# GpSimd instead of ScalarE writes the normalised rows after attention

## The chip, the cores and the metric

The kernel is one program on one core of a Trainium2 chip. The metric is the device time of one execution in microseconds (us). A core has five engines that run their own instruction streams and meet at semaphores: TensorE (PE; PEld is its weight load), VectorE (DVE), ScalarE (ACT), GpSimd (POOL) and SyncE (SP), which here only issues DMAs.

## The reference, cut to what matters

Two blocks, each a cross attention and an expert layer, on x of 4 x 1024 rows of 256 and a context of 4 x 64 rows of 192:

```python
x = x + xattn0(_layernorm(x), ctx, mask, ...)      # 8 heads of 64
x = x + ffn0(_layernorm(x), Wr, W1, W2)            # top 1 of 8 experts, with a capacity
x = x + xattn1(_layernorm(x), ctx, ...)            # 16 heads of 64
x = x + ffn1(_layernorm(x), Wg, W11, W12, W2)      # top 2 of 8 experts, gated

def _layernorm(x, axis=-1, eps=1e-05):
    m = jnp.mean(x, axis=axis, keepdims=True)
    v = jnp.var(x, axis=axis, keepdims=True)
    return (x - m) / jnp.sqrt(v + eps)
```

The change concerns the second and the fourth `_layernorm`, those on the sum of x and attention's output. Their result is what the router reads and what is sent to the experts.

## The kernel before, in words

The 4096 rows are 32 tiles (NT) of 128 rows. `attention(p, layer, ...)` is called once for each layer. Each engine has a function in it that loops over the same counter t, from -8 to 36, and does in round t a different step for different tiles: a software pipeline whose order is written out by hand. In round t:

- PE (`tensor`) transposes the softmax of tile t (L691), the normalised input of tile t + 4 (L700) and the normalised result of tile t - 2 (L706), makes the scores of tile t + 3 (L719), the output of tile t (L739) and the router's logits of tile t - 2 (L745), and for every fourth tile counts ranks (L755 to L759).
- DVE (`vector`) adds the output to x for tile t - 1 (L1091), takes the row maxima of tile t + 2 (L1119) and the statistics of tile t - 1 and of tile t + 6 (L1123 to L1145), and runs small steps of routing between them.
- ACT (`scalar`) copies transposes out of PSUM (L773, L777, L780), takes the exponentials of tile t + 2 (L794, one instruction a head and a read of its sum), and last in the round, for tile t - 1, writes the normalised rows (L804): x times 1/std plus a bias.
- POOL (`gpsimd`) scales the softmax of tile t + 1 by the reciprocal of its sum (L832), in the second layer fetches the expert rows of tile t + 8 (L840), sends a finished tile to the experts' buffer by one indirect DMA in the first layer and two in the second (L816), and then makes var + eps (L852), its power of -1/2 (L854) and that bias, -mean/std (L857).

So in round t the rows of tile t - 1 go DVE, POOL, ACT, and are read by PE in round t + 1. In the first layer they go to `L_stage`, a ring of 12 tiles; in the second they overwrite x in place, once the store of x to the output (issued by SP, L635) has landed. The scatter of tile u is issued 10 rounds (second layer 9) after its round by `scattered_at`, tighter for the last tiles; from round NT - 3 on it stands behind the variance steps and not ahead of them. The experts' stage of the second layer starts inside the last rounds (`behind`), with the gate of `E_sg` on ACT.

Names in the rows: `L_prob` softmax, `L_mv` mean and variance, `L_rstd` 1/std, `L_nb` the bias, `L_got` fetched expert rows, `rows` the experts' buffer in memory, `L_rcp` reciprocal of the sums.

## Time and profile before

| | us |
|---|---|
| time, median of 3 runs (lowest to highest) | 1082.34 (1081.46 to 1084.64) |
| span of the profiled execution | 1076.3 |
| first attention, from its first scores to the last tile | about 40 to 200 |
| first experts | about 200 to 500 |
| second attention | about 500 to 740 |
| second experts | about 740 to 1076 |

The span runs from the first to the last instruction; the 6.0 us between it and the median are start and end of the execution, outside all instructions. No time of its own is given for the profiled execution, so its span plus these 6.0 us stands for it, which by this definition is the median. In the stretch 40 to 200 PE is busy 155.0 of 160.0 us, in 500 to 740 it is 235.3 of 240.0. In the second stretch ACT is busy 214.9 and POOL 171.6 us.

How to read it: a row of the timeline has the start, the duration, the engine, the line and the operands, and in brackets how long the engine stood idle before it and what ended that. Indirect DMAs count as busy for POOL, but the gaps between them are issue time, in which POOL does nothing else either.

### The profile page before, as it was taken

What the parts mean: (1) busy time and instruction counts of PE and PEld (TensorE: products, weight loads), DVE (VectorE), ACT (ScalarE), POOL (GpSimd) and SP (SyncE); (2) the same over time, 40 slices, a digit from 0 to 9 for tenths busy, and PEclk for the clock granted to TensorE, in tenths of its full rate; (3) what the DMA queues carried; (4) which work ended last, traced back from release to release, by engine and by line L of the source; (5) the groups of instructions that cost most, each with busy time, mean ns of one, the idle gap of its engine ahead of it and who ended that gap; (6) DMA issues with size and microseconds to landing.
All of it is one profiled execution on the core that took longest, in us unless ns stands there. A gap on an engine that the chain in (4) does not pass through costs nothing.

```text
span 1076.3 us, 24183 instructions
## 1 busy us (share of the span) xinstructions
PE 1022.2 (95%) x7550; PEld 945.6 (88%) x7550; DVE 715.1 (66%) x2216; ACT 660.2 (61%) x2446; POOL 514.3 (48%) x522
## 2 busy tenths in 40 slices
PE   6999999899999999988999999989999999999994
PEld 4688888699999999866999999889899999999994
DVE  6778886454554444475777777858967676677663
ACT  2788987454554444347999999886445454444441
POOL 1356776442223333324558888766634324333233
PEclk9999999799999999988999999999999999999997
DMA  9920000466667775500111222247898566875783
GB/s 313 345 92 21 31 26 31 152 244 224 218 234 244 244 263 186 173 20 16 36 40 65 79 74 70 91 138 248 238 307 233 129 193 164 291 210 116 215 259 34
DMA packets 95490, 169.71 MB, mean 158 GB/s; under 512 B 12322, under 2 KB 70308, under 8 KB 93860
## 3 DMA queue, kind: packets, MB, share of 16 engines
q1 hardware_dynamic: 79028, 142.33, 39.0%
q0 software_dynamic: 16368, 26.23, 11.2%
q8 instruction: 46, 0.75, 0.3%
q14 instruction: 48, 0.39, 0.1%
HBM read 150.67 MB, written 62.43 MB: 198 GB/s over the span
## 4 chain that ended last, share of the span: by engine, by line
PE 77%; DVE 8%; DMA 7%; ACT 3%; issue 3%; POOL 1%; SPq 0%; POOLq 0%; DVEq 0%; ACTq 0%
PE psum L1720 13%; PE psum L719 11%; PE psum L739 11%; PE psum L1302 10%; PE psum L1319 10%; PE psum L1774 5%; PE psum L691 3%; DMA out<-E_y,E_dest 3%; PE psum L392 2%; ACT L_prob L794 2%; DMA E_up_w<-up 2%; PE psum L745 2%; PE psum L355 1%; PE psum L706 1%; PE psum L1740 1%
## 5 line engine op out<-in xcount | busy, mean ns | idle before, releaser
L794 ACT ACTIVATE L_prob<-psum,L_neg_max 128x64 f32<-128x64 f32 x768 | 228.6, 361 | 4.7 <-DVE L_neg_max L1119 4.6
L794 ACT ACTIVATION_READ_ACCUMULATOR L_prob<-psum,L_neg_max 128x1 f32 x768 | 194.8, 256 | 0.0
L1720 PE MATMUL psum<-E_xT_hi,E_up_w 128*128 128x256 f32 x1024 | 187.7, 281 | 6.7 <-DMA E_up_w<-up 3.3
L2131 POOL DMA_INDIRECT out<-E_y,E_dest x64 | 104.9, 1639 | 166.0 <-DVE E_y L1989 69.0
L1720 PEld LDWEIGHTS psum<-E_xT_hi,E_up_w 128*128 128x128 f32 x1024 | 158.4, 188 | 9.2 <-issue 7.5
L1720 PE MATMUL psum<-E_xT_lo,E_up_w 128*128 128x256 f32 x512 | 142.7, 279 | 0.0
L1874 ACT ACTIVATE E_sg<-psum 128x256 f32<-128x256 f32 x128 | 48.5, 382 | 107.8 <-PE psum L1720 106.2
L832 POOL TENSOR_TENSOR L_prob<-L_prob,L_rcp 128x512 f32<-128x512 f32 (+1 forms) x64 | 94.3, 1474 | 42.2 <-DVE L_rcp L1083 40.8
L739 PE MATMUL psum<-L_n_hi,L_pT_hi 128*128 128x256 f32 x384 | 107.5, 280 | 3.4 <-DVE L_pT_lo L1126 3.4
L1360 ACT ACTIVATE E_h_hi<-psum 128x256 fp32r<-128x256 f32 (+1 forms) x128 | 55.6, 437 | 85.8 <-PE psum L1302 85.8
L739 PE MATMUL psum<-L_n_lo,L_pT_hi 128*128 128x256 f32 x384 | 106.6, 277 | 0.0
L739 PE MATMUL psum<-L_n_hi,L_pT_lo 128*128 128x256 f32 x384 | 106.5, 277 | 0.0
L1403 DVE SCALAR_TENSOR_TENSOR E_h_lo<-psum,E_h_hi 128x256 fp32r<-128x256 f32 (+1 forms) x128 | 62.6, 491 | 54.2 <-ACT E_h_hi L1360 53.6
L1720 PEld LDWEIGHTS psum<-E_xT_lo,E_up_w 128*128 128x128 f32 x512 | 96.1, 188 | 0.0
L1319 PE MATMUL psum<-E_w_hi,E_h_hi 128*128 128x256 f32 x320 | 90.0, 281 | 0.0
L1319 PE MATMUL psum<-E_w_lo,E_h_hi 128*128 128x256 f32 x320 | 89.4, 279 | 0.0
L1319 PE MATMUL psum<-E_w_hi,E_h_lo 128*128 128x256 f32 x320 | 89.4, 279 | 0.0
L719 PE MATMUL psum<-L_m_hi,L_xT_hi 128*128 128x512 f32 x192 | 82.9, 432 | 2.0 <-ACT L_prob L794 2.0
L1302 PE MATMUL psum<-E_xT_hi,E_w_hi 128*128 128x384 f32 (+1 forms) x256 | 78.8, 308 | 1.4 <-DVE E_xT_lo L1395 1.4
L1302 PE MATMUL psum<-E_xT_hi,E_w_lo 128*128 128x384 f32 (+1 forms) x256 | 78.8, 308 | 0.0
L1302 PE MATMUL psum<-E_xT_lo,E_w_hi 128*128 128x384 f32 (+1 forms) x256 | 78.7, 308 | 0.0
L1952 DVE TENSOR_TENSOR E_hf<-psum,E_sg 128x256 f32<-128x256 f32 x128 | 53.5, 420 | 37.9 <-ACT E_sg L1874 37.8
(278 smaller groups left out, 3120.8 us busy)
## 6 DMA issues: line engine op xcount, KB each, us to landing
E_up_w<-up SPq DMA_DIRECT2D x26, 2048.0 KB
E_w<-in_w SPq DMA_DIRECT2D x16, 1024.0 KB, 7.2
E_w<-in_w SPq DMA_DIRECT2D x29, 512.0 KB
E_half_up_w<-up SPq DMA_DIRECT2D x28, 512.0 KB, 6.1
E_xin<-rows SPq DMA_DIRECT2D x32, 260.0 KB, 3.4
E_raw<-in_w SPq DMA_DIRECT2D x16, 512.0 KB, 7.0
up<-E_raw_hi SPq DMA_DIRECT2D x16, 512.0 KB, 6.5
up<-E_raw_lo SPq DMA_DIRECT2D x16, 512.0 KB, 3.7
```

The source lines that it names most:

```text
L719: mm = e.matmul(bank, a[:, (t + 3) % 2, c, :], m[:, b, c, q * 512:(q + 1) * 512], start=(layer == 1 and c == 0 and j == 0), stop=(c == KC ...
L739: mm = e.matmul(o, a[:, r, :], m[:, b, r, :], start=(r == 0 and j == 0), stop=(r == PR - 1 and j == 2))
L794: last = e.activation(prob[q][:, h * KEYS:(h + 1) * KEYS], scores_ps(t)[:, h * KEYS:(h + 1) * KEYS], ACT.Exp, bias=nmx[:, q, h, :], accum_ ...
L832: e.tensor_tensor(pr, pr, rc[:, q, :, :].to_broadcast([P, H, KEYS]), ALU.mult).then_inc(s_p, 1)
L1302: mm = q.matmul(bank, a[par][:, c, m * P:(m + 1) * P], x[:, c, c0 * P:(c0 + cn) * P], start=(k == 0), stop=(k == 3 * KC - 1))
L1319: mm = q.matmul(bank, a[:, h, m, c * P:(c + 1) * P], w[par][:, m, :], start=(k == 0), stop=(k == 3 * FC - 1))
L1360: q.activation(h_hi[:, h, m, 0:cn * P], ps[:, UP_BANK + m % 4, 0:cn * P], ACT.Relu).then_inc(s_hhi, 1)
L1403: q.scalar_tensor_tensor(h_lo[:, h, m, 0:cn * P], ps[:, UP_BANK + m % 4, 0:cn * P], 0.0, h_hi[:, h, m, 0:cn * P].bitcast(F32), ALU.max, AL ...
L1720: mm = q.matmul(bank, up_w[wpar(i, par)][:, half, w, c, m * P:(m + 1) * P], x[:, c, :], start=(k == 0), stop=(k == 3 * KC - 1))
L1774: mm = q.matmul(ps[:, Y_BANK + c, 0:D], a[:, par, m, c * P:(c + 1) * P], w[:, b, m, :], start=(k == 0), stop=(k == 3 * FC - 1))
L1952: q.tensor_tensor(hf[:, m, :], ps[:, UP_BANK + m, T1:2 * T1], sg[:, m, :], ALU.mult).then_inc(s_hf, 1)
L2131: q.indirect_dma_start(p.out[:, :], bass.IndirectOffsetOnAxis(ap=dest[:, par, c, :], axis=0), y[:, par, c, :], None, compute_op=ALU.add).t ...
```

## The change

For each of the 64 tiles, POOL's third small instruction (the bias, 128x1) becomes the pass over the rows itself, 128x256: subtract the mean, multiply by 1/std. ACT's pass and the bias tile go. The waits for the place that is written (in the first layer the ring slot's scatter, in the second the store of x) move with the pass from ACT's queue to POOL's. PE gets one more wait, in the first layer's round NT - 2: the banks of the last scores are about to be reused there, and until now ACT's pass told that its exponentials had been taken.

```diff
@@ attention: tensor
+            if ahead and t == NT - 2:
+                need(e, s_exp, NT)
@@ attention: scalar
-            if ok(t - 1):
-                i = t % 4
-                need(e, s_nb2, t)
-                if layer == 0:
-                    need(e, s_scat[(t - 1) % RING], 16 * ((t - 1) // RING))
-                else:
-                    need(e, s_store[(t - 1) % 4], 16 * ((t - 1) // 4 + 1))
-                e.activation(rows2(t - 1), p.x[:, t - 1, 0:D], ACT.Identity, bias=nb2[:, i:i + 1],
-                             scale=rs[:, i, 0:1]).then_inc(s_xf, 1)
@@ attention: gpsimd
                 if ok(t - 1):
                     need(e, s_rs, nrs(t))
-                    e.tensor_scalar(nb2[:, i:i + 1], mv[:, i, 0, 0:1], -1.0, rs[:, i, 0:1],
-                                    ALU.mult, ALU.mult).then_inc(s_nb2, 1)
+                    if layer == 0:
+                        need(e, s_scat[(t - 1) % RING], 16 * ((t - 1) // RING))
+                    else:
+                        need(e, s_store[(t - 1) % 4], 16 * ((t - 1) // 4 + 1))
+                    e.tensor_scalar(rows2(t - 1), p.x[:, t - 1, 0:D], mv[:, i, 0, 0:1], rs[:, i, 0:1],
+                                    ALU.subtract, ALU.mult).then_inc(s_xf, 1)
```

POOL's queue in a middle round of the second attention, before (the number behind a buffer's name tells its copies apart; in brackets the semaphores waited for):

```order
L852 TENSOR_SCALAR L_var_eps<-L_mv 128x2 [waits mean_var1,mean_var2]
L854 TENSOR_TENSOR L_rstd<-L_var_eps,half 128x2 [waits var_eps]
L857 TENSOR_SCALAR L_nb_150<-L_mv,L_rstd 128x1 [waits rstd]
L832 TENSOR_TENSOR L_prob_138<-L_prob_138,L_rcp 128x1024 [waits reciprocal]
L840 DMA L_got<-rows,row 128x256 [waits combined]
L816 DMA rows<-x,L_row_167 35072x260 [waits xf,routing]
```

and in the same round now:

```order
L844 TENSOR_SCALAR L_var_eps<-L_mv 128x2 [waits mean_var1,mean_var2]
L846 TENSOR_TENSOR L_rstd<-L_var_eps,half 128x2 [waits var_eps]
L853 TENSOR_SCALAR x<-x,L_mv,L_rstd 128x256 [waits x_stored3,rstd]
L824 TENSOR_TENSOR L_prob_137<-L_prob_137,L_rcp 128x1024 [waits reciprocal]
L832 DMA L_got<-rows,row 128x256 [waits combined]
L808 DMA rows<-x,L_row_165 35072x260 [waits xf,routing]
```

One instruction has changed its size, from one column to 256, and waits for a store as well; the order is the same. A second scatter follows in both.

ACT's queue in the same stretch, before:

```order
L794 ACTIVATE L_prob_139,L_sum<-psum,L_neg_max 128x64 x15
L804 ACTIVATE x<-x,L_nb_150,L_rstd 128x256 [waits x_stored0,neg_mean2]
L773 ACTIVATE L_pT_hi<-psum 128x1024 [waits pT]
L777 ACTIVATE L_xT_hi<-psum 128x256 [waits xfT,xT]
L780 ACTIVATE L_xfT<-psum 128x256 [waits xfT]
```

and now:

```order
L795 ACTIVATE L_prob_138,L_sum<-psum,L_neg_max 128x64 x15
L774 ACTIVATE L_pT_hi<-psum 128x1024 [waits pT]
L778 ACTIVATE L_xT_hi<-psum 128x256 [waits xfT,xT]
L781 ACTIVATE L_xfT<-psum 128x256 [waits xfT]
```

The pass between the exponentials and the copy of the transposed softmax is gone, and with it ACT's only wait for POOL in a round. DVE's and SP's queues and the order of PE's are as they were.

## Rows read from the trace of the kernel before

**Rows 1.** The chain that ended last, second attention: start, us, what.

```profile
573.06 0.93 PE psum L691 x8
...
574.20 0.32 PE psum L706 x2
...
668.27 0.94 PE psum L691 x8
```

**Rows 2.** PE's waits ahead of L706, first attention: total us, times.

```profile
ACT L_stage L804: 2.6, 9
```

**Rows 3.** POOL's waits in the stretch 40 to 200: total us, times, longest.

```profile
POOL L_var_eps L852 <- DVE L_mv L1145: 33.7, 26, 2.4
```

**Rows 4.** POOL's timeline over a round of the second attention, and a later row.

```profile
572.00 0.22 POOL L852 TENSOR_SCALAR L_var_eps<-L_mv 128x2 f32<-128x2 f32 x1
572.30 0.72 POOL L854 TENSOR_TENSOR L_rstd<-L_var_eps,half 128x2 f32<-128x2 f32 x1
573.14 0.26 POOL L857 TENSOR_SCALAR L_nb<-L_mv,L_rstd 128x1 f32<-128x1 f32 x1
573.44 1.90 POOL L832 TENSOR_TENSOR L_prob<-L_prob,L_rcp 128x1024 f32<-128x1024 f32 x1
575.51 1.07 POOL L840 DMA_INDIRECT L_got<-rows,row  x1 [0.17 <-issue]
576.88 1.00 POOL L816 DMA_INDIRECT rows<-x,L_row  x1 [0.30 <-DVE L_r L879]
578.19 0.97 POOL L816 DMA_INDIRECT rows<-x,L_row  x1 [0.30 <-issue]
579.23 0.23 POOL L852 TENSOR_SCALAR L_var_eps<-L_mv 128x2 f32<-128x2 f32 x1
...
667.10 0.23 POOL L852 TENSOR_SCALAR L_var_eps<-L_mv 128x2 f32<-128x2 f32 x1
```

**Rows 5.** Groups by line, shapes apart: count | busy us, mean ns | idle before.

```profile
L832 POOL TENSOR_TENSOR L_prob<-L_prob,L_rcp 128x1024 f32<-128x1024 f32 x32 | 60.9, 1904 | 33.6 <-DVE L_rcp L1083 32.8
L1440 POOL TENSOR_TENSOR E_raw_lo<-E_raw,E_raw_hi 128x1024 fp32r<-128x1024 f32 x16 | 38.4, 2403 | 76.6 <-ACT E_raw_hi L1369 70.1 <-DMA up<-E_raw_lo 6.6
L832 POOL TENSOR_TENSOR L_prob<-L_prob,L_rcp 128x512 f32<-128x512 f32 x32 | 33.4, 1043 | 8.6 <-DVE L_rcp L1083 8.0
L857 POOL TENSOR_SCALAR L_nb<-L_mv,L_rstd 128x1 f32<-128x1 f32 x64 | 17.3, 270 | 7.1
L339 POOL MEMSET L_vd<- 128x4096 f32 x1 | 3.5, 3512 | 0.0
```

**Rows 6.** ACT's waits in the stretch 515 to 740: total us, times, longest.

```profile
ACT x L804 <- POOL L_nb L857: 11.5, 18, 4.1
ACT x L804 <- DMA out<-x: 1.2, 1, 1.2
```

**Rows 7.** The chain again, at 196 and at 699 us.

```profile
196.49 0.50 ACT L_stage L804
...
698.78 0.58 POOL L_rstd L854
...
699.77 0.61 ACT x L804
```

**Rows 8.** POOL's timeline at the first attention's last tile.

```profile
193.73 0.57 POOL L854 TENSOR_TENSOR L_rstd<-L_var_eps,half 128x1 f32<-128x1 f32 x1
```

**Rows 9.** PE's timeline at the same place and at 722 us.

```profile
197.12 0.66 PE L706 MATMUL psum<-ident,L_stage 128*128 128x128 f32 x2 [0.60 <-ACT L_stage L804]
...
722.26 0.41 PE L706 MATMUL psum<-ident,x 128*128 128x128 f32 x2 [0.37 <-ACT x L804]
```

**Rows 10.** DVE's timeline: one small step away from L832 and beside it.

```profile
635.58 0.19 DVE L880 TENSOR_TENSOR L_sh<-L_lg,L_r 128x32 f32<-128x32 f32 x1
...
724.48 1.64 DVE L880 TENSOR_TENSOR L_sh<-L_lg,L_r 128x32 f32<-128x32 f32 x1
```

**Rows 11.** Busy us of each engine in one stretch, granted clock, DMA share.

```profile
735.00:745.00 10.00, 10.00 (x96) 10.00 (x96) 7.23 (x22) 6.24 (x17) 5.25 (x7) 1.00 0.54 150
```

More of the change, by code:

```diff
@@ L510, in attention @@
     rs = small("rstd", [P, 4, 2])
-    nb2 = small("nb2", [P, 4])
     if layer == 1:
@@ L556, in attention @@
     s_bn1, s_ag1, s_bn2, s_ag2 = S("stats1"), S("mean_var1"), S("stats2"), S("mean_var2")
-    s_eps, s_rs, s_nb2 = S("var_eps"), S("rstd"), S("neg_mean2")
+    s_eps, s_rs = S("var_eps"), S("rstd")
     s_xn, s_xT, s_xThi, s_xTlo = S("xn"), S("xT"), S("xT_hi"), S("xT_lo")
@@ L1171, in attention @@
     st.EARLY_TABLE, st.PLAN_STEPS = EARLY_TABLE, PLAN_STEPS
-    st.done = {s: NT for s in (s_bn1, s_ag1, s_bn2, s_ag2, s_nb2, s_xn, s_xT, s_xThi, s_xTlo, s_sim, s_mx, s_exp, s_rcp, s_p,
+    st.done = {s: NT for s in (s_bn1, s_ag1, s_bn2, s_ag2, s_xn, s_xT, s_xThi, s_xTlo, s_sim, s_mx, s_exp, s_rcp, s_p,
                                s_pT, s_pThi, s_pTlo, s_out, s_res, s_xf, s_xfT, s_xfTc, s_lgp, s_lg)}
```

## The prediction

> **What bounds the kernel now.** I read first the chain of work that ended last, in order of time, over both attentions. In the second it is one PE group after another, round upon round: L691 starts at 573.06 and, 13 rounds later, at 668.27 [rows 1], so a round is 95.21 / 13 = 7.32 us, PE's own work with next to no wait in it. In the first attention it reads the same. Next I asked who PE waits for ahead of L706, the transposes of the rows in question: 2.6 us in 9 waits in the first attention [rows 2], and in the second at single places late in it. That is all PE loses to ACT's pass today, and so about all that a pass finished sooner can give back. ACT is off this path, and its 64 passes of 0.6 us are hidden.
>
> Then POOL, which takes the work. In the first attention it has room: it stood 33.7 us over 26 rounds, 1.3 us in each, waiting for DVE's statistics [rows 3]. In the second, in the rounds that hold a fetch and two scatters, it has none: from 572.00 to 579.23 each instruction follows the last with only issue gaps [rows 4], 7.23 us of work in a round of 7.32; from 572.00 to 667.10 are 13 rounds of 7.315. POOL is full there, 0.09 us a round below PE. This is where the change is decided.
>
> **The length of the new pass, X.** No row has a two-operation tensor_scalar of 256 columns on POOL. Its fixed part is in L857, the same instruction on one column: 0.27 us [rows 5]. For the columns there are three slopes. A memset runs 4096 columns in 3.51 us, 0.86 ns each, and nothing that reads and writes should be faster: 0.27 + 256 x 0.86 ns = 0.48 us at least. The two-input multiply L832 goes from 1.043 us at 512 columns to 1.904 at 1024, 1.68 ns a column: 0.69 us. The two-input subtract into fp32r takes 2.403 us for 1024 columns, 2.35 ns each: 0.87 us, the upper end. The pass has one input and plain fp32 output, so I stand near the low end, for the second operation a little above it: X = 0.55 us. The Trainium skill's page GPSIMD Engine Reference, section Engine selection, bears on this: two-input elementwise operations cost GpSimd about twice VectorE's time and one-input ones run roughly at line rate; its section on the performance per element gives 1.03 cycles at 1.2 GHz for bodies of at most two operations. By this X would be 0.49, and the sum below 0.9 us lower. The same page's section 7 speaks against the change: an fp32 dependent chain, as subtract then multiply is, would cost 4 cycles an element. That would be 0.85 us on top of the fixed part and X = 1.12; no row here shows such a slope, the steepest being 2.35 ns.
>
> **Removed on ACT:** 64 passes and their waits for POOL (in the second attention 11.5 us in 18 waits [rows 6]). They are beside PE's work: ACT's next step, L773, needs PE's L691, which ends after the exponentials anyway (L691 runs from 573.06 to 573.99 [rows 1]). Worth 0 in itself. What the passes delay is L706, next.
>
> **Rows sooner for PE.** Today, at 698.78, L_rstd takes 0.58, L_nb and the pass follow, and the rows are there at 700.38 [rows 7]: 1.02 us after L_rstd. In the change it is 0.11 (the gap from L854 to L857 at 573.02 to 573.14 [rows 4]) plus X, 0.66 us. So 0.36 us sooner wherever this chain is what PE waits for.
> - First attention: 8 waits of L706, 2.0 us together (2.6 [rows 2] less the 0.60 of the one at 197 [rows 9]), 0.25 each in the mean, so under the 0.36; all but part of the longest goes: -1.7.
> - The wait at 196: ACT does its pass at 196.49 [rows 7] only because it is behind other work; POOL's L_rstd ended at 194.30 [rows 8]. PE waits 0.60 there, and the whole chain to the last scatters and the experts' first rows hangs on it: -0.5, with a little left for what is late next, the rank counts.
> - Second attention: at 699.77 -0.35; at 722 ACT's pass stands behind its exponentials and PE waits 0.37 [rows 9], which goes whole: -0.37.
> Sum -2.9 us. POOL's own round in the first attention grows by X - 0.27 = 0.28, and the 1.3 us of idle time hide it.
>
> **POOL's full rounds.** Each grows by X - 0.265 from 7.23 to 7.515 us [rows 4], against PE's 7.30 without its few small waits. PE does not feel it at once. At 573 the rows would be ready at 573.02 + 0.11 + 0.55 = 573.68, and L706 wants them at 574.20 [rows 1] less 0.05 of signalling: 0.47 in hand. After that PE gets a new wait of 0.21 ahead of L706 in each round. There are 14 such rounds (9 to 23; from round 24 on there is no fetch, which takes 1.37 us out of POOL's round, and POOL idles again): 14 x 0.215 - 0.47 = +2.5 us. In general that is 14 (X - 0.335) - (1.02 - X). What is queued behind the longer pass is L832, whose result PE needs only a round later, with 5 us in hand (575.34 against 573.06 + 7.32), and the fetch and scatters, which nobody awaits in these rounds. PE's time lost here doesn't come back, as PE has no idle time to give.
>
> **The waits that move.** In the second attention the pass waits for the store of x. Only once did ACT wait for it, 1.2 us at the last tile [rows 6]; elsewhere the store has landed in time. POOL will wait that about 1 us instead, with the scatters of tiles 28 and 29 and then the first adds of experts' output behind it. Those adds wait for DVE's E_y anyway, which covers it: 0, or 1 us if that cover is gone. PE's new wait for s_exp is for exponentials finished a round before: 0.
>
> **A rule against it.** DVE's small L880 takes 0.19 us normally and 1.64 when it starts inside an L832 [rows 10]: two engines on SBUF can hold each other off. The Trainium skill's page SBUF — State Buffer, section Who interferes with whom, gives the reason: a DVE instruction with two SBUF inputs shares GpSimd's read port, and the second to issue blocks until the first finishes; the trace agrees. In the full rounds the pass and the shifted L832 (now ending about 0.7 us later) fall beside DVE steps that read PSUM or one SBUF operand, and the next with two SBUF inputs, L1134, comes just behind. DVE also waits for ACT's sums in each round, which absorbs a hit. I count 0, with up to +2 in the range.
>
> **Sum:** -2.9 + 2.5 = -0.4 us on 1076.3 + 6.0, which gives 1081.9; I say 1082.0.
>
> **The rivals.**
> - *GpSimd becomes the bound in earnest (slower).* The pass runs at the slope of L1440 [rows 5], X = 0.87. The full rounds give 14 x 0.535 - 0.15 = +7.3; of the gains only 1.7 stay (0.8 in the first attention, 0.5 at 196, 0.37 at 721). Sum +5.6: 1088. With X = 0.69 it is 4.6 - 2.7 = +1.9. It costs more than 3.2 us from X = about 0.76 on. For it: subtract-then-multiply may be two steps of a loop. Against: one input. Were every column to wait for both operations in turn, at a slope of 3.3 ns that no row here has, X would be 1.12 and the time 14 x 0.785 + 0.1 = 11.1 later less 1 or so of gains, 1092; I give that 0.03 of this rival's 0.25. (That is what the rule on dependent chains in the Trainium skill's page GPSIMD Engine Reference, section 7, would make of the pass.)
> - *ACT's freedom pays at the seam (faster).* Around 727 to 741 us ACT stands in front of its pass, up to 4.1 us for POOL and 1.2 for the store [rows 6], and the gates of the second experts, E_sg, queue behind it; right after them the chain goes through DVE. If DVE's work there starts 2.5 us sooner and X = 0.48 (-1.5), the time is 1078.3. For it: the waits are real. Against: PE is busy 10.00 of 10.00 us from 735 to 745 [rows 11], so its PSUM results, not ACT, time these steps.
> - *The full rounds don't bind and only gains stay:* if the issue gaps around the DMAs shrink as the pass grows, -2.9: 1079.4. Against: the 0.30 us gap is the same from row to row [rows 4].
>
> **How the numbers follow.** The forecast, X between 0.48 and 0.75, has 0.60: 1080.8 to 1085. GpSimd as the bound 0.25. The seam 0.09, gains alone 0.06. Within 0.3%, 3.2 us, about what a measurement of this kernel can tell from no change, lies the forecast; of the last case's 1079.4 nearly all is inside too, of the slower rival's a little. Faster 0.12, same 0.62, slower 0.26. The range of 8 in 10 is 1079.5 to 1088.0.
>
> **What would show it.** The new POOL pass at 0.5 to 0.6 us, 64 times. Rounds of the second attention from 573 to 668 of 7.5 us, with waits of PE ahead of L706 on POOL of about 0.2 us in each; POOL without idle time there. In the first attention no waits ahead of L706, and the first experts starting about 2 us sooner. ACT's idle time moved ahead of L773. Wrong would be: a pass above 0.75 us, full rounds that stay at 7.32, or a change of more than 1 us in the stretch after 745.

## The result, and the profile after

The changed kernel takes **1102.18 us** (median of 4 runs, 1098.03 to 1103.07), the kernel before, run beside it, 1083.49 us (4 runs, 1081.46 to 1088.41). The ratio is 1.0158, 95% interval 1.0126 to 1.0190: by the ratio 17 us slower, by the two medians 18.7. The prediction was 1082.0 with a range of 1079.5 to 1088.0, and "same" as the likeliest. It is wrong, in sign and in size.

The first thing to read is the new pass itself. The two groups of the changed kernel, shapes apart (count | busy us, mean ns | idle before), are:

```profile
L853 POOL TENSOR_SCALAR x<-x,L_mv,L_rstd 128x256 f32<-128x256 f32 x32 | 40.9, 1279 | 5.0 <-DMA out<-x 1.7
L853 POOL TENSOR_SCALAR L_stage<-x,L_mv,L_rstd 128x256 f32<-128x256 f32 x32 | 39.5, 1233 | 3.5
```

X is 1.23 us, not 0.55, and above the upper bound of 0.87 that the prediction took from the rows of before. Most of the loss follows from it. The full round of the second attention that answers to [rows 4] now reads on POOL (start us, us, instruction):

```profile
574.45 0.25 POOL L844 TENSOR_SCALAR L_var_eps<-L_mv 128x2 f32<-128x2 f32 x1
574.78 0.72 POOL L846 TENSOR_TENSOR L_rstd<-L_var_eps,half 128x2 f32<-128x2 f32 x1
575.62 1.23 POOL L853 TENSOR_SCALAR x<-x,L_mv,L_rstd 128x256 f32<-128x256 f32 x1
576.82 1.90 POOL L824 TENSOR_TENSOR L_prob<-L_prob,L_rcp 128x1024 f32<-128x1024 f32 x1
578.89 1.30 POOL L832 DMA_INDIRECT L_got<-rows,row  x1 [0.18 <-issue]
580.50 1.01 POOL L808 DMA_INDIRECT rows<-x,L_row  x1 [0.30 <-DVE x L878]
581.81 0.97 POOL L808 DMA_INDIRECT rows<-x,L_row  x1 [0.30 <-issue]
582.81 0.26 POOL L844 TENSOR_SCALAR L_var_eps<-L_mv 128x2 f32<-128x2 f32 x1
```

There is again no idle time but the issue gaps, and the round is 8.36 us here and 8.18 in the mean of the 14 such rounds, against 7.31 before. The chain, which went from one PE group to the next [rows 1], now goes through POOL (start us, us, what):

```profile
583.16 0.72 POOL L_rstd L846
583.99 1.24 POOL x L853
585.27 0.44 PE psum L705 x2
...
600.40 1.24 POOL x L853
601.68 0.44 PE psum L705 x2
...
616.69 1.24 POOL x L853
617.97 0.44 PE psum L705 x2
```

Two rounds lie between these PE groups: 585.27 to 601.68 to 617.97, 16.4 and 16.3 us. In between the chain runs over PE's scores and output, DVE's steps and POOL's two scatters. From 572 to 690 us PE's matmuls wait for POOL ahead of L705 14 times, 8.6 us together; before, the same stretch shows no wait of theirs. Over the whole kernel the idle time of PE and its weight load ahead of that line reads

```profile
POOL x L853: 25.5, 33
POOL L_stage L853: 7.7, 21
```

where before it was 2.6 us in 9 waits in the first attention [rows 2]. (Idle time of matmuls and of weight loads is added up here, so one gap can count twice.) Shares of the chain were PE 77%, DVE 8%, POOL 1% and are now:

```profile
PE 67%; DVE 13%; POOL 7%; issue 5%; DMA 4%; ACT 3%; POOLq 0%; DVEq 0%; SPq 0%; ACTq 0%
```

In the first attention POOL's wait for DVE's statistics was 33.7 us in 26 waits before [rows 3]; from 40 to 200 us it is now 15.3 us in 19 waits. Of the two rounds below the first has 0.40 us of it left, the second nothing:

```profile
122.92 0.23 POOL L844 TENSOR_SCALAR L_var_eps<-L_mv 128x2 f32<-128x2 f32 x1 [0.40 <-DVE L_mv L1141]
123.23 0.72 POOL L846 TENSOR_TENSOR L_rstd<-L_var_eps,half 128x2 f32<-128x2 f32 x1
124.06 1.23 POOL L853 TENSOR_SCALAR L_stage<-x,L_mv,L_rstd 128x256 f32<-128x256 f32 x1
125.27 1.03 POOL L824 TENSOR_TENSOR L_prob<-L_prob,L_rcp 128x512 f32<-128x512 f32 x1
126.48 1.10 POOL L808 DMA_INDIRECT rows<-L_stage,row  x1 [0.18 <-issue]
127.61 0.40 POOL L844 TENSOR_SCALAR L_var_eps<-L_mv 128x2 f32<-128x2 f32 x1
```

**Where the time went.** Four places of the timeline divide the span. "First experts" and "second experts" are the starts of the experts' first transposes of E_xin on PE; "24 rounds" runs from the first L_var_eps of two columns in the second attention to the last L_rstd of two columns, 24 rounds later; "experts' length" is from the first to the last start of the second experts' matmuls with E_up_w. All in us; a second trace of each of the two kernels (see the experiments) stands in the table too. A row is one execution, and that can lie 10 us from its kernel's median: the traced run of "one operation" took 1083.79 us, the fastest of five with a median of 1093.64.

| kernel | first experts | 24 rounds | second experts | experts' length | span |
|---|---|---|---|---|---|
| before | 214.0 | 176.5 | 715.1 | 334.8 | 1076.3 |
| before, second trace | 213.1 | 176.5 | 710.9 | 330.9 | 1068.5 |
| after | 218.5 | 188.3 | 729.8 | 339.6 | 1095.3 |
| after, second trace | 219.3 | 188.2 | 730.6 | 346.5 | 1104.9 |
| one operation | 214.1 | 184.5 | 719.4 | 337 | 1082.0 |
| constants | 217.4 | 186.4 | 730.4 | 344 | 1100.5 |
| two halves | 226.7 | 193.5 | 747.6 | 340 | 1113.5 |
| second attention only | 214.5 | 188.3 | 725.9 | 344 | 1096.2 |
| extra pass beside | 214.4 | 191.6 | 729.0 | 345 | 1100.7 |
| VectorE, both | 212.0 | 177.9 | 713.4 | 339.5 | 1082.8 |
| VectorE, first only | 214.9 | 176.4 | 715.3 | 344 | 1087.6 |
| first attention only | 219.1 | 176.8 | 720.6 | 336.0 | 1082.9 |
| softmax shared | 218.4 | 179.9 | 721.2 | 334.0 | 1081.3 |
| last seven tiles only | 213.7 | 176.5 | 711.9 | 332.9 | 1071.9 |

Of the 19.0 us between the first two spans, 4.5 come in the first attention, 11.8 in the 24 rounds, and 4.8 in the second experts' stretch; the rest of the kernel gives 2.1 back. The first two are sharp: the 24 rounds repeat within 0.1 us from trace to trace. The start of the first experts lies between 213.1 and 214.5 us in the five traces with the first attention of before, between 218.4 and 219.3 in the four with that of after. The experts' length is not sharp: it moves by 4 us between two traces of before and by 7 between two of after, and "VectorE, first only", whose second attention is that of before, has 344.

### The profile page after: what moved, and what is told of

It is laid out like the page before. It is cut to its first block, busy times and chain, and to the rows that moved or that the text cites. A ratio compares the mean times of both kernels' runs of the same rounds, so it can differ in the third digit from the quotient of the medians.

```text
span 1095.3 us, 24120 instructions
## 1 busy us (share of the span) xinstructions
PE 1024.7 (94%) x7550; PEld 942.4 (86%) x7550; DVE 722.8 (66%) x2216; ACT 627.3 (57%) x2382; POOL 579.4 (53%) x522
## 4 chain that ended last, share of the span: by engine, by line
PE 67%; DVE 13%; POOL 7%; issue 5%; DMA 4%; ACT 3%; POOLq 0%; DVEq 0%; SPq 0%; ACTq 0%
PE psum L1716 13%; PE psum L1298 10%; PE psum L1315 10%; PE psum L718 7%; PE psum L740 7%; PE psum L1770 6%; DMA out<-E_y,E_dest 3%; ACT L_prob L795 2%; PE psum L355 2%; DVE L_neg_max L1115 2%; POOL rows L808 2%; PE psum L392 2%; DVE L_pT_lo L1122 2%; POOL L_rstd L846 1%; PE psum L690 1%
## 5 line engine op out<-in xcount | busy, mean ns | idle before, releaser
L824 POOL TENSOR_TENSOR L_prob<-L_prob,L_rcp 128x512 f32<-128x512 f32 (+1 forms) x64 | 94.1, 1470 | 23.7 <-DVE L_rcp L1079 23.7
L774 ACT ACTIVATE L_pT_hi<-psum 128x512 fp32r<-128x512 f32 (+1 forms) x64 | 52.0, 813 | 75.5 <-PE psum L690 75.5
L1430 POOL TENSOR_TENSOR E_w_lo<-E_w,E_w_hi 128x2048 fp32r<-128x2048 f32 x8 | 38.9, 4865 | 76.7 <-ACT E_w_hi L1339 76.7
```

Source lines behind the costliest of these rows:

```text
L774: e.activation(flat(pT_hi[:, :, :]), pT_ps(), ACT.Copy).then_inc(s_pThi, 1)
L824: e.tensor_tensor(pr, pr, rc[:, q, :, :].to_broadcast([P, H, KEYS]), ALU.mult).then_inc(s_p, 1)
```

## The experiments

Two theories stood against each other at first. By **occupancy**, POOL has no room in its rounds, so any longer instruction there lengthens the round, whatever it computes. By **latency**, the rows themselves come later than by the bias on GpSimd and the pass on ScalarE, so PE's transposes wait for them, and other work on POOL doesn't matter. Beside them stood the question what makes the pass 1.23 us long, and whether VectorE could have done it.

**One operation.** The mean is not subtracted, so the rows are only scaled.

```diff
-e.tensor_scalar(rows2(t - 1), p.x[:, t - 1, 0:D], mv[:, i, 0, 0:1], rs[:, i, 0:1],
-                ALU.subtract, ALU.mult).then_inc(s_xf, 1)
+e.tensor_scalar(rows2(t - 1), p.x[:, t - 1, 0:D], rs[:, i, 0:1], None,
+                ALU.mult).then_inc(s_xf, 1)
```

> The pass on GpSimd with one operation in place of two: multiply by 1/std, the mean is not subtracted (left out of the computation; it is near 0). My theory T1: the pass took 1.23 us, not 0.55, because the two operations on an element are done one after the other on each column, 3.8 ns a column; with one of them it goes to about half of that, 0.27 + 256 x 1.9 ns = 0.75 us, and the time to within 3 us of before (1082 to 1088). Rival T2: the cost is that of a read and a write of fp32 with scalars from memory, whatever the operations; the pass stays at 1.2 us and the time at the changed kernel's 1098 to 1103.

Measured: 1093.64 us, ratio 1.0081 (1.0060 to 1.0102). The pass is

```profile
L853 POOL TENSOR_SCALAR x<-x,L_rstd 128x256 f32<-128x256 f32 x32 | 31.5, 985 | 4.3 <-DMA out<-x 1.1
L853 POOL TENSOR_SCALAR L_stage<-x,L_rstd 128x256 f32<-128x256 f32 x32 | 30.1, 941 | 3.3
```

0.29 us shorter in the first attention: so much is the second operation worth together with its per-partition operand, the mean. In the second attention it is 0.94 as well, except for one of 2.16 us at the end, which lifts the mean to 0.985. Neither theory of the expectation, 0.75 or 1.2 us, holds, and even one operation takes more than the prediction's upper bound for two. The time, some 9 us above before, is not within the 3 us that were expected. The first attention now loses nothing (first experts at 214.1), the 24 rounds lose 8.0 us. So the first attention does hide a pass of 0.94 us; it does not hide 1.23.

**Constants.** Two operations, with 0.0 and 1.0 in place of the mean and the reciprocal; the rows are not normalised.

```diff
-e.tensor_scalar(rows2(t - 1), p.x[:, t - 1, 0:D], mv[:, i, 0, 0:1], rs[:, i, 0:1],
+e.tensor_scalar(rows2(t - 1), p.x[:, t - 1, 0:D], 0.0, 1.0,
                 ALU.subtract, ALU.mult).then_inc(s_xf, 1)
```

> Both operations stay, but with the constants 0.0 and 1.0 in place of the per-row mean and 1/std (the rows are not normalised). T1 (the two operations one after the other): the pass stays near 1.2 us and the time near that of the changed kernel. T3: what is slow is taking two scalars per row from memory; then the pass falls to 0.5 to 0.7 us and the time to within 3 us of before.

Measured: 1099.35 us, ratio 1.0115 (1.0070 to 1.0160). The pass takes

```profile
L853 POOL TENSOR_SCALAR x<-x 128x256 f32<-128x256 f32 x32 | 35.6, 1112 | 4.3 <-DMA out<-x 1.5
L853 POOL TENSOR_SCALAR L_stage<-x 128x256 f32<-128x256 f32 x32 | 34.7, 1085 | 2.8
```

so the two per-partition operands are worth 0.15 us of the 1.23 (again without the last pass, 1.90 us here). With 0.07 for one operand the second operation alone is some 0.22 us, an estimate from these two kernels. T3, a fall to 0.5 to 0.7, is wrong. The rows, and so the routing, are others here and in "one operation"; what is compared are the pass and the rounds.

**Two halves.** The pass in two instructions of 128 columns.

```diff
-e.tensor_scalar(rows2(t - 1), p.x[:, t - 1, 0:D], mv[:, i, 0, 0:1], rs[:, i, 0:1],
-                ALU.subtract, ALU.mult).then_inc(s_xf, 1)
+for c in range(2):
+    h = slice(c * P, (c + 1) * P)
+    last = e.tensor_scalar(rows2(t - 1)[:, h], p.x[:, t - 1, h], mv[:, i, 0, 0:1], rs[:, i, 0:1],
+                           ALU.subtract, ALU.mult)
+last.then_inc(s_xf, 1)
```

> The pass in two instructions of 128 columns each, the same result. It gives slope and fixed part: if the fixed part is the 0.27 us of the one-column instruction and the slope 3.8 ns, each half takes 0.75 us and the pair 1.5. GpSimd's full rounds in the second attention then go from 8.17 to 8.4 or 8.5 us, and by 14 full rounds and some in the first attention the kernel is 5 to 8 us slower than the changed one (T1: GpSimd's occupancy is the bound). If instead the fixed part is large (0.7 us or more), each half takes nearly 1 us and the kernel is over 12 us slower. If GpSimd's occupancy is not the bound, the time stays.

Measured: 1115.95 us, ratio 1.0291 (1.0267 to 1.0314). Each half:

```profile
L855 POOL TENSOR_SCALAR x<-x,L_mv,L_rstd 128x128 f32<-128x128 f32 x64 | 52.7, 831 | 3.4 <-DMA out<-x 0.2
L855 POOL TENSOR_SCALAR L_stage<-x,L_mv,L_rstd 128x128 f32<-128x128 f32 x64 | 50.9, 803 | 3.3
```

From 128 to 256 columns the pass grows by (1233 - 803) / 128 = 3.36 ns a column, and 1.233 - 256 x 0.00336 = 0.37 us is fixed. (The one-column instruction took 0.27 [rows 5], so the line is not quite straight.) The full rounds are 8.51 us, the 24 rounds 5.2 us longer than in the changed kernel, the first experts start 8.2 us later. By the ratios that is some 14 us in all, where 5 to 8 were expected; what was left too small is the first attention. The prediction said of a slope of 3.3 ns that no row had it; the steepest there was 2.35 [rows 5]. The Trainium skill's page GPSIMD Engine Reference, section 7, gives 4 cycles an element to an fp32 dependent chain, which the prediction put at X = 1.12 with its own fixed part of 0.27; the trace agrees with the size of that slope. That such a chain is the cause is not shown: the pass with constants has the same two operations in turn, and with the same fixed part its 1.085 us give 2.8 ns a column, the single operation's 0.94 give 2.2 (estimates from these rows). The same page's section Engine selection, by which one-input operations run roughly at line rate, and its 1.03 cycles an element, from which the prediction worked out 0.49, do not agree: even with one operation the pass takes 0.94.

**Second attention only.** ScalarE and the bias are back in the first attention.

```diff
# ScalarE's pass
-if ok(t - 1):
+if ok(t - 1) and layer == 0:
# GpSimd
+if layer == 0:
     e.tensor_scalar(nb2[:, i:i + 1], mv[:, i, 0, 0:1], -1.0, rs[:, i, 0:1], ALU.mult, ALU.mult).then_inc(s_nb2, 1)
+else:
+    need(e, s_store[(t - 1) % 4], 16 * ((t - 1) // 4 + 1))
+    e.tensor_scalar(rows2(t - 1), p.x[:, t - 1, 0:D], mv[:, i, 0, 0:1], rs[:, i, 0:1], ALU.subtract, ALU.mult).then_inc(s_xf, 1)
```

> The change in the second attention alone; the first attention is as before. Of the 19 us, my reading of the two traces puts 4.5 in the first attention and the rest from 500 us on: then this kernel is 13 to 15 us slower than before, with the first experts' first transposes at 214 us as before. If the first attention's loss were larger than it looks because its delay is made good or doubled later, it would come out below 11 or above 18.

Measured: 1097.54 us, ratio 1.0098 (1.0071 to 1.0125). First experts at 214.5, as before; the 24 rounds 188.3, as in the changed kernel. The second attention has its loss without the first. By the ratio the time is 10.6 us above before (7.7 to 13.6), below the 13 to 15 that were expected, which the interval just reaches.

**Extra pass beside.** The kernel before, with its bias and ScalarE's pass, and on GpSimd, for 28 tiles of the second attention, one more pass of the new kind over a constant tile, which nobody waits for.

```diff
     e.tensor_scalar(nb2[:, i:i + 1], ...).then_inc(s_nb2, 1)
+    if layer == 1 and t < NT - 3:
+        e.tensor_scalar(scratch[:, :, :], p.ident[:, None, :].to_broadcast([P, 2, P]), mv[:, i, 0, 0:1], rs[:, i, 0:1],
+                        ALU.subtract, ALU.mult)
```

> The kernel before, with ScalarE's pass and GpSimd's small bias kept, and in the second attention (28 of its 32 tiles) one more GpSimd pass of the same form, 128x256 subtract and multiply, that reads a constant tile and writes scratch nobody reads. It stands behind the bias, so the rows for TensorE are not made later by it directly. T1 (GpSimd's occupancy is the bound in the full rounds): the pass takes 1.23 us, a full round 8.2 + 0.3 us (the bias stays in it), and the kernel is 11 to 15 us slower than before. T4 (what costs is the longer way from 1/std to the rows, 1.34 us in place of 1.02, round by round): under 3 us slower.

Measured: 1101.72 us, ratio 1.0162 (1.0102 to 1.0222). The extra pass, whose result goes nowhere, takes as long and lengthens the rounds to 8.42 us:

```profile
578.45 0.27 POOL L858 TENSOR_SCALAR L_nb<-L_mv,L_rstd 128x1 f32<-128x1 f32 x1
578.69 1.24 POOL L861 TENSOR_SCALAR L_scratch<-ident,L_mv,L_rstd 128x256 f32<-128x256 f32 x1
579.90 1.91 POOL L833 TENSOR_TENSOR L_prob<-L_prob,L_rcp 128x1024 f32<-128x1024 f32 x1
```

The 24 rounds take 191.6 us, 15.1 more than before, 3.3 more than in the changed kernel, which has no bias of 0.27 us in its 14 full rounds (3.8 us). This decides for occupancy and against latency in the second attention: the rows come from ScalarE as ever, and the loss is there. The time, 17.5 us above before by the ratio (11.0 to 24.0), is more than the 11 to 15 that were expected; in the trace the experts' length is 345 too, 10 above the first of before.

**VectorE, both attentions.** VectorE writes the rows right behind its own reciprocal; neither ScalarE's pass nor the bias is left.

```diff
# VectorE
     e.reciprocal(rc[:, q, :, :], sm[:, q, :, :]).then_inc(s_rcp, 1)
+if ok(t - 2):
+    u, i = t - 2, (t - 1) % 4
+    need(e, s_rs, nrs(t - 1))
+    ...
+    e.tensor_scalar(rows2(u), p.x[:, u, 0:D], mv[:, i, 0, 0:1], rs[:, i, 0:1], ALU.subtract, ALU.mult).then_inc(s_xf, 1)
# GpSimd and ScalarE
-e.tensor_scalar(nb2[:, i:i + 1], ...)
-e.activation(rows2(t - 1), ...)
```

> A version that might beat both: VectorE writes the rows, behind its reciprocal, one instruction of 128x256 like its L_xn (0.41 us), and neither ScalarE's pass nor GpSimd's bias is left. The way from 1/std to the rows is 0.1 + 0.41 us against 1.02 before, GpSimd's full round falls from 7.23 to 6.93 us, and VectorE's round grows by 0.33 us, of which it has 1 us and more idle. T1 and T4 both expect 1 to 4 us faster than before, by the small waits of TensorE ahead of its transposes. Rival T5: VectorE's later maxima and differences delay TensorE, or its serial stretch from 724 to 768 us grows by some passes: 1 to 5 us slower.

Measured: 1089.61 us (12 runs), ratio 1.0036 (1.0004 to 1.0069). The gain that was expected isn't there; the time is inside the range of rival T5. On VectorE the same pass takes a third of the time or less:

```profile
L1079 DVE TENSOR_SCALAR x<-x,L_mv,L_rstd 128x256 f32<-128x256 f32 x32 | 14.0, 438 | 0.9 <-POOL L_rstd L846 0.7 <-issue 0.2
L1079 DVE TENSOR_SCALAR L_stage<-x,L_mv,L_rstd 128x256 f32<-128x256 f32 x32 | 12.4, 387 | 0.0
```

One pass of 1.99 us lifts the first mean; the middle one is 0.33 us there and 0.38 into L_stage. The first experts start at 212.0, 2.0 us sooner; the 24 rounds take 177.9, 1.4 more than before. So VectorE could carry the work at a small cost, 0.4 to 7.5 us by the interval, and no gain showed. PE is busy 196.1 of the 200 us from 510 to 710, before 198.5. What makes the rest of the 3.9 us was not separated.

**A second trace of before, first attention only, softmax shared, last seven tiles.** These four ran beside the same runs of before. The first is the kernel before, unchanged.

> The kernel before, unchanged, for a second trace of it. In the first trace the second experts' matmuls ran from 722.4 to 1057.2 us, 334.8 us long, and in the changed kernel they took 339.6. If that stretch varies from one execution to the next by itself, a second trace of the same kernel shows it 3 to 10 us longer than 334.8 while the attentions before it stay within 1 us (first experts from 214.0, second experts' transposes from 715.1); then the 5 us of the changed kernel after 745 us are not all the change's. If the stretch is fixed, it is again 334.5 to 335.5, and the 5 us belong to the change.

Measured: span 1068.5 us. The experts' length is 330.9 us, 3.9 shorter, not longer as was thought likely, and the second experts start 4.2 us sooner although the 24 rounds are the same 176.5. Both stretches thus vary by some 4 us from one execution to the next. That is nearly as much as the 4.8 us which the changed kernel seemed to lose behind its attention.

*First attention only* is the reverse of "second attention only" (`layer == 1` in place of `layer == 0`, and the wait for s_scat with the pass).

> GpSimd writes the rows in the first attention alone; the second is as before. Occupancy theory: POOL's round in the first attention grows from 3.3 of work in 4.6 us by 0.96, its 1.3 us of idle time almost go, and its loop with DVE and PE becomes the longest: the first experts start at 218 to 219 us instead of 214.0, and the time is 3.5 to 6.5 us above before. Rival, that 1.3 us of idle time hide 0.96 and only the second attention costs: the first experts within 1 us of 214.0 and the time within 1 us of before.

Measured: 1081.48 us (12 runs), ratio 1.0035 (1.0011 to 1.0060), 3.8 us. First experts at 219.1, the 24 rounds 176.8. This is the loss of the first attention by itself, and with the 1.0098 of its complement it makes 1.0133, inside the interval of the whole. The rival, that 1.3 us of idle time in each round hide the pass, is wrong.

POOL's timeline of the first attention shows why, read over the 24 rounds with L_var_eps of two columns, 111.8 us before and 116.0 after. In the kernel before, POOL waited 1.6 to 2.6 us in each of the first eight of them, which hold no scatter, but only 0.73 to 1.17 us in the other sixteen, under 0.96 in eleven of these. In the sixteen, 3.0 us are lost, and POOL is left with 0 to 0.42 us of waiting. The other 1.2 us are lost in the first eight, in which POOL still waits 0.5 to 2.0 us. There, in the changed kernel, the chain goes from DVE's statistics through L_rstd and the pass to PE's L705 (62.55 and 71.97 us), so by the chain what costs there is that the rows come later, not that POOL is full. In the first attention both theories thus seem to have a part; no experiment separates them there.

*Softmax shared* is the changed kernel, in which VectorE scales half of the softmax rows in rounds 9 to 23 of the second attention.

```diff
# GpSimd
-e.tensor_tensor(pr, pr, rc[:, q, :, :].to_broadcast([P, H, KEYS]), ALU.mult).then_inc(s_p, 1)
+n_h = H // 2 if shared(t) else H
+e.tensor_tensor(pr[:, 0:n_h, :], pr[:, 0:n_h, :], rc[:, q, 0:n_h, :].to_broadcast([P, n_h, KEYS]), ALU.mult).then_inc(s_p, 1)
# VectorE, at the end of its round
+if shared(t):
+    e.tensor_tensor(pr, pr, rc[:, q, H // 2:H, :].to_broadcast([P, H // 2, KEYS]), ALU.mult).then_inc(s_half, 1)
```

> The changed kernel, but in rounds 9 to 23 of the second attention VectorE scales the second half of the softmax rows (8 of 16 heads) at the end of its round, so GpSimd's multiply is of 512 columns and 0.86 us shorter there; the pass by GpSimd stays. Occupancy theory: GpSimd's full round falls from 8.15 to 7.3 to 7.5 us, PE is again the bound, the second experts' transposes start 9 to 11 us sooner than in the changed kernel (729.8), at 719 to 721 us, and the time is 8 to 11 us below the changed kernel. Rival, that the rows come too late for PE (latency of subtract and multiply) whatever else GpSimd does: rounds stay at 8.0 or more and the time within 3 us of the changed kernel. Rival, that VectorE has no room: its round becomes the bound at 7.6 to 7.9 and only half of the time comes back.

Measured: 1087.95 us, ratio 1.0101 (1.0058 to 1.0143). POOL's round is shorter again:

```profile
574.01 0.72 POOL L852 TENSOR_TENSOR L_rstd<-L_var_eps,half 128x2 f32<-128x2 f32 x1
574.85 1.23 POOL L859 TENSOR_SCALAR x<-x,L_mv,L_rstd 128x256 f32<-128x256 f32 x1
576.05 1.03 POOL L829 TENSOR_TENSOR L_prob<-L_prob,L_rcp 128x512 f32<-128x512 f32 x1
...
581.29 0.74 POOL L852 TENSOR_TENSOR L_rstd<-L_var_eps,half 128x2 f32<-128x2 f32 x1
...
588.60 1.24 POOL L852 TENSOR_TENSOR L_rstd<-L_var_eps,half 128x2 f32<-128x2 f32 x1
...
596.11 0.80 POOL L850 TENSOR_SCALAR L_var_eps<-L_mv 128x2 f32<-128x2 f32 x1
...
596.15 0.69 DVE L1166 TENSOR_TENSOR L_prob<-L_prob,L_rcp 128x512 f32<-128x512 f32 x1
```

The two rounds here are 7.3 us long, but the mean of the 14 full rounds is 7.61 (7.27 to 8.23). The 24 rounds take 179.9 instead of 188.3, and the second experts start at 721.2, 8.6 us sooner, with the pass still on GpSimd. Some 3.4 of 11.8 us do not come back. The last two rows show where: while DVE scales its half of the softmax, a small POOL instruction beside it takes longer. L_var_eps takes 6.65 us over the 14 full rounds, 0.26 each in the changed kernel, so 3.0 us more; L_rstd took 1.24 instead of 0.72 once. POOL still stands idle only in issue gaps, while DVE waits 14.8 us for ACT's exponentials from 572 to 690 us. So the rival that VectorE has no room has the length of the rounds right, 7.6, but not the reason: POOL is still the full engine. The span is 14 us below the changed kernel's, but the traced run was the fastest of its six; the ratio is only 0.6% lower (some 6 us, and with overlapping intervals), less than the 8 to 11 that were expected. So the rounds confirm the cause, and the size in total time is only roughly confirmed.

*Last seven tiles only*: GpSimd writes the rows of tiles 25 to 31 of the second attention, with the moved wait for the store; everything else is as before.

```diff
-if ok(t - 1):                                   # ScalarE's pass
+if ok(t - 1) and not (layer == 1 and t >= 26):
...
+need(e, s_store[(t - 1) % 4], 16 * ((t - 1) // 4 + 1))      # GpSimd, for t >= 26
+need(e, s_xf, t - 1)
+e.tensor_scalar(rows2(t - 1), p.x[:, t - 1, 0:D], mv[:, i, 0, 0:1], rs[:, i, 0:1], ALU.subtract, ALU.mult).then_inc(s_xf, 1)
```

> GpSimd writes the rows of tiles 25 to 31 of the second attention alone, with the moved wait for the store of x; all other rows are ScalarE's, as before. It shows the seam by itself. Theory that the moved wait and the stretched pass at the seam cost time: the second experts' transposes start 2 to 4 us later than the 715.1 of before, and the time is 2 to 5 us above it. Rival, that all of the loss lies in the full rounds and the first attention: the transposes within 1 us of 715.1 and the time within 1.5 us of before.

Measured: 1075.07 us (12 runs), ratio 0.9996 (0.9969 to 1.0024). The moved wait and the last seven passes cost nothing that can be measured, though in the changed kernel's trace they look costly. There the chain reads

```profile
751.77 3.17 DMA out<-x
...
755.11 2.46 POOL x L853
...
757.71 0.42 PE psum L705 x2
```

and it is true that POOL waits 1.66 us for the store and that the pass is stretched to twice its length. But rows on a chain are not yet lost time: PE is busy 5.79 of the 5.93 us from 751.77 to 757.70, with experts' matmuls. In the trace of "last seven tiles only" POOL stands idle 1.25 us at that place and the pass takes 2.52 us, and the time is that of before.

**A second trace of after, and VectorE in the first attention only.** The first is the changed kernel, unchanged.

> The changed kernel, unchanged, for a second trace of it. In its first trace TensorE's last rank counts ran from 765.0 to 770.8 us with 4.7 us of gaps marked issue between matmuls that take 0.17 us each, and the second experts' matmuls took 339.6 us against 334.8 and 330.9 in two traces of before. If these gaps are accidents of one execution, they are gone or elsewhere here and the stretch is 331 to 337 us. If they belong to the changed order of work, they are again 3 us or more at the same matmuls and the stretch is 338 to 342. The attentions must repeat in either case: the pass 1.23 us, full rounds of 8.15 us, the first experts from 218.5 us and the second experts' transposes 11 to 12 us after their place in the kernel before less what differs before round 9.

Measured: span 1104.9 us. The attentions repeat; the experts' length is 346.5 us, above both ranges of the expectation. What was to be told apart is the last rank counts. In the kernel before, eight matmuls on PE follow each other within 0.4 us:

```profile
750.41 0.19 PE L755 MATMUL psum<-L_oh_b,below 128*128 128x32 bf16 x1
750.45 0.22 PE L757 MATMUL psum<-L_oh_b,ones_b 128*128 128x24 bf16 x3
750.52 0.24 PE L759 MATMUL psum<-L_oh_b,ones_b 128*128 128x8 bf16 x4
```

In the first trace of the changed kernel they take from 765.00 to 770.81:

```profile
765.00 0.18 PE L756 MATMUL psum<-L_oh_b,below 128*128 128x32 bf16 x1 [0.22 <-DVE L_oh_b L890]
765.59 0.17 PE L758 MATMUL psum<-L_oh_b,ones_b 128*128 128x24 bf16 x1 [0.41 <-issue]
767.70 0.17 PE L758 MATMUL psum<-L_oh_b,ones_b 128*128 128x16 bf16 x1 [1.94 <-issue]
769.13 0.17 PE L758 MATMUL psum<-L_oh_b,ones_b 128*128 128x8 bf16 x1 [1.26 <-issue]
```

and in the second trace:

```profile
767.90 0.18 PE L756 MATMUL psum<-L_oh_b,below 128*128 128x32 bf16 x1 [1.80 <-issue]
769.34 0.17 PE L758 MATMUL psum<-L_oh_b,ones_b 128*128 128x24 bf16 x1 [1.26 <-issue]
770.73 0.17 PE L758 MATMUL psum<-L_oh_b,ones_b 128*128 128x16 bf16 x1 [1.22 <-issue]
```

The gaps repeat (4.7 and 4.9 us in all), so they are no accident of one execution. "Second attention only" has them too (4.9 us), "constants" half (2.4), and 2.0 ahead of the matmuls before them. In the other kernels the rank counts themselves have none, but gaps marked issue stand ahead of other matmuls in the 12 us before their last rank count: 3.4 us in "one operation", 3.5 in "two halves", 2.9 in "extra pass beside", 0.9 in "VectorE, both", and 2.9 in "VectorE, first only", whose second attention is that of before. The two traces of before, "first attention only", "softmax shared" and "last seven tiles only" have none there. So neither the pass on GpSimd nor the late end of the attention is needed for them. What PE waits for there no row shows. DMA is busy in full at the time (share 1.04, 401 GB/s from 765 to 771), but in the softmax-shared kernel it is as well (1.02, 368 GB/s from 753 to 759), without gaps, so that alone isn't it.

The gaps are not all that they cost. PE was busy 1.27 of the 6 us from 765 to 771; after that its granted clock was 0.50, the 1.2 GHz level, from 771 to 773 us, and 1.00 again from 774. In the second trace it was 0.50 from 771 to 777. Over the experts' length PE stood idle 12.9 us in the first trace of the changed kernel and 8.8 in the first of before, which is 4.1 of the 4.8 us. This part of the loss stays open: how much of it is the change's, and what sets the experts' length, 331 to 347 us over all these traces.

*VectorE in the first attention only* has the edit of "VectorE, both" under `layer == 0`.

> VectorE writes the rows in the first attention, next to its own reciprocal, with no bias on GpSimd there and no pass on ScalarE; the second attention is as before. When VectorE wrote the rows in both, the first experts started at 212.0 us instead of 214.0 but the second attention gave it back. If the first attention's gain stands by itself, the first experts start at 211.5 to 212.5 us, the second attention is as before, and the time is 1 to 2.5 us below before (ratio 0.9975 to 0.999), a version that is ahead of both kernels. Rival, that the first experts' or second attention's start is held by something else and takes the gain back: within 0.5 us of before.

Measured: 1084.47 us (12 runs), ratio 1.0022 (0.9996 to 1.0047), no gain. The first experts start at 214.9, not at 212; in this trace PE has one gap of 1.6 us marked issue ahead of L706 in the first attention and waits 0.9 us for the experts' first rows. No version was found that beats the kernel before.

## Why the prediction was wrong

- **The step that failed is "The length of the new pass, X".** It took 0.55 us, bounds 0.48 to 0.87; measured 1.23. (By its own terms, 0.27 + 0.22 and 0.27 + 0.43, the lower two values are 0.49 and 0.70, not 0.48 and 0.69; nothing hangs on that.) The bounds came from a memset and from two-input operations of other widths, and were read as if "one input, plain output" must be cheaper than "two inputs". The columns cost 3.36 ns each, above the steepest slope in the trace, 2.35. The one value that was near, 1.12, had a chance of 0.03 of the whole, because no row showed its slope. That a row doesn't show an operation is no evidence that it is cheap. X accounts for the full rounds; the prediction's own formula for them gives 1095 with the true X and none of the gains, so the first attention and the experts' length make the rest.
- **The full rounds: mechanism right.** POOL full, PE waiting ahead of L705 in each round, no idle time, all as forecast. The formula 14 (X - 0.335) - (1.02 - X) gives +12.7 us with X = 1.23; measured are 11.8 over the 24 rounds. With 0.94 (one operation) it gives 8.4 against 8.0, with 1.085 (constants) 10.6 against 9.9, with 1.60 (two halves) 18.3 against 17.0. So it is 0.4 to 1.3 us too high, and its slope is right within about a tenth.
- **"POOL's own round in the first attention grows by 0.28, and the 1.3 us of idle time hide it": wrong with the true X.** It grows by 0.96. That is still under 1.3, and yet the loss is 4.5 us in the trace and 3.8 in the time of the kernel with this part alone. The 1.3 was a mean over 26 waits in two kinds of rounds, of which the sixteen with scatters had 0.73 to 1.17 us, and in the first eight rounds the later rows cost time although POOL was idle (see "first attention only"). The 24 rounds there grew by 0.4 us with a pass of 0.94, by 2.0 with 1.085, by 4.2 with 1.23 and by 10.0 with two halves of 0.80.
- **Rows sooner for PE, -2.9 us: not there.** L_rstd to rows ready is now 0.11 + 1.23 = 1.34 us, against 1.02 before. The gain of each tile was tied to X below 0.9.
- **The waits that move, 0: confirmed in time** (ratio 0.9996), though the trace shows 1.66 us of wait on POOL at that place.
- **Contention, "I count 0, with up to +2":** it occurs. DVE's two-input L876, 0.19 us normally [rows 10], took 2.55, to 741.51, when POOL's L824 ran from 739.53 to 741.45:

```profile
738.96 2.55 DVE L876 TENSOR_TENSOR L_sh<-L_lg,L_r 128x32 f32<-128x32 f32 x1
```

  and the last pass, beside two-input steps of DVE from 754.73 on, took twice its length:

```profile
755.11 2.45 POOL L853 TENSOR_SCALAR x<-x,L_mv,L_rstd 128x256 f32<-128x256 f32 x1 [1.66 <-DMA out<-x]
```

  Both lie at the end of the attention, where the experiment with the last seven tiles finds no loss.
- **The 6.0 us outside the span** were an error of reading. The span belonged to one short execution, the median to others. The runs that have both numbers show 1.7 to 3.4 us outside the span; the changed kernel's profiled run took 1098.03 with a span of 1095.3. Adding 6 to the span gave the median of before by definition, so it moved no difference between the kernels, but it hid that executions differ by some 10 us.
- **The slower rival** named the mechanism that came true, with X = 0.87 and 1088 us. It had a chance of 0.25 and the wrong size: of the 17 us the full rounds give 11.8, and it counted 7.3.

## What to carry to other kernels

Before work is given to GpSimd, find its duration there in a trace, or treat it as unknown up to the dearest rule at hand; a two-operation fp32 tensor_scalar of 128 x 256 took 1.23 us there, and 0.33 to 0.38 on VectorE. Where an engine that isn't the bound has only 0.1 us left in a round, every instruction added to it lengthens every round, and a pass that nobody reads is the cleanest way to show it. Idle time is to be read round by round: a mean of 1.3 us hid that most rounds with a scatter had under 0.96. A chain that ends last is a path and not a bill: a step on it, doubled, may still be worth nothing, and only a kernel with that step alone tells.

## What the runs showed of the hardware

- GpSimd, fp32, 128 partitions: tensor_scalar with two operations and per-partition operands took 0.27 us on 1 column (one operand a constant there), 0.80 on 128, 1.23 on 256; with one operation on 256, 0.94; with two constants 1.085. Beside two-input steps of VectorE a single pass took up to twice as long.
- VectorE did the 256 columns in 0.38 (into L_stage) and 0.33 us (in place, on x), the middle of 32 each.
- Once VectorE scaled half of the softmax in the same rounds, L_var_eps on GpSimd (2 columns) went from 0.26 to up to 0.80 us, L_rstd from 0.72 to 1.24 at one place.
- Eight small matmuls that took 0.4 us in one kernel took 5.8 in another with the same code there, with gaps of 0.4 to 1.9 us between them that no semaphore explains. After them TensorE's granted clock was 0.50 for 2 to 6 us.
